# A two-layer attention kernel: the first unit's scores in larger tiles, and an earlier count for the scores made ahead

## What is computed

```python
xn = layernorm(x, g_in)
q = (xn @ Wq).reshape(b, n, H, DH).transpose(0, 2, 1, 3) * scale
k, v = split(xn @ Wkv)            # one head; a null key and value in front
sim = einsum('bhid,bjd->bhij', q, k) + bias
sim = where(causal | padded, -max, sim)
out = einsum('bhij,bjd->bhid', softmax(sim), v)
x = x + layernorm(out.reshape(b, n, H * DH) @ Wo, g_out)
# then the same form again as layer 1
```

## Time and profile before

| what | us |
|---|---|
| median of three runs | 2392.63 (2391.18 to 2395.41) |
| profiled execution | 2398.92 |
| its span | 2397.1 |
| PE busy | 2148.4 |
| DVE, ACT, POOL busy | 1624.3, 1557.8, 1030.0 |

### The profile page before, as it was taken

The page is one execution under the profiler, slowest core; times in us unless marked ns, Lnnn a source line. Parts: engine busy times, 40 slices in busy tenths (PEclk is TensorE's granted clock), DMA queues, the critical chain, the costliest instruction groups (busy, mean ns, idle before and its releaser), DMA issues.

```text
span 2397.1 us, 72132 instructions
## 1 busy us (share of the span) xinstructions
PE 2148.4 (90%) x26395; PEld 1914.7 (80%) x26395; DVE 1624.3 (68%) x3422; ACT 1557.8 (65%) x6241; POOL 1030.0 (43%) x1510
## 2 busy tenths in 40 slices
PE   5898988899988989888999889899899998898987
PEld 4787887788877878877888778778788887787876
DVE  5776766666766767666666666676666666676775
ACT  4676666666666766666666666666666666666765
POOL 3444444444444444444444444444444444444443
PEclk8899999999999999999999999999999999999999
DMA  7121222221222212222212211222122122211211
GB/s 244 50 58 54 63 60 59 63 60 53 58 69 58 57 52 65 57 59 63 60 53 58 69 59 53 55 58 65 59 59 65 53 58 64 59 57 53 69 49 51
DMA packets 183286, 151.60 MB, mean 63 GB/s; under 512 B 121440, under 2 KB 125616, under 8 KB 182992
## 3 DMA queue, kind: packets, MB, share of 16 engines
q1 hardware_dynamic: 181248, 145.77, 20.7%
q0 software_dynamic: 688, 1.14, 0.3%
q10 hardware_dynamic: 1056, 0.00, 0.0%
HBM read 98.56 MB, written 37.77 MB: 57 GB/s over the span
## 4 chain that ended last, share of the span: by engine, by line
PE 84%; issue 8%; DVE 2%; ACT 2%; SPq 1%; POOL 1%; DMA 1%; DVEq 0%; POOLq 0%; ACTq 0%
PE psum L708 31%; PE psum L615 17%; PE psum L581 12%; PE psum L673 9%; PE psum L691 7%; PE psum L543 3%; PE psum L632 2%; PE psum L592 2%; DVE bn_in L1072 1%; SPq L386 1%; ACT qp L870 1%; POOL probs L1474 1%; POOL masked_bias L1464 0%; ACT ln_in L839 0%; ACT probs L900 0%
## 5 line engine op out<-in xcount | busy, mean ns | idle before, releaser
L900 ACT ACTIVATE probs<-probs,neg_max 128x129 f32<-128x129 f32 (+3 forms) x2048 | 712.1, 351 | 76.3 <-DVE neg_max L1140 76.2
L1464 POOL TENSOR_TENSOR masked_bias<-bias,pad_neg 128x516 f32<-128x516 f32 (+3 forms) x512 | 404.1, 821 | 349.0 <-DVE probs L1134 345.3
L1474 POOL TENSOR_TENSOR probs<-probs,den_inv 128x512 f32<-128x512 f32 (+3 forms) x512 | 367.8, 739 | 250.3 <-DVE den_inv L1145 250.3
L1134 DVE TENSOR_TENSOR probs<-psum,masked_bias 128x648 f32<-128x648 f32 x256 | 213.0, 832 | 313.3 <-PE psum L673 312.8
L1486 POOL TENSOR_TENSOR y_out<-y_out,res 128x512 f32<-128x512 f32 x128 | 164.6, 1286 | 554.5 <-ACT y_out L864 554.5
L900 ACT ACTIVATION_READ_ACCUMULATOR probs<-probs,neg_max 128x1 f32 x2048 | 385.9, 188 | 0.0
L1150 DVE STREAM_TRANSPOSE probs_t<-probs 128x512 f32<-128x512 f32 (+3 forms) x512 | 229.9, 487 | 147.3 <-POOL probs L1474 146.3
L708 PE MATMUL psum<-wo_hi,o_hi 128*128 128x512 f32 x1024 | 307.0, 447 | 3.6 <-issue 2.1
L906 ACT ACTIVATE o_hi<-psum,null_v_col 128x512 fp32r<-128x512 f32 x256 | 161.9, 683 | 196.2 <-PE psum L691 196.2
L673 PE MATMUL psum<-keys,q_t 64*64 64x129 f32 (+3 forms) x4096 | 129.6, 265 | 156.0 <-issue 152.9
L708 PE MATMUL psum<-wo_hi,o_lo 128*128 128x512 f32 x1024 | 262.5, 398 | 0.0
(11 more groups left out here) (133 smaller groups left out, 4077.0 us busy)
## 6 DMA issues: line engine op xcount, KB each, us to landing
res<-in_x_dram SPq DMA_DIRECT2D x64, 256.0 KB, 2.8
v_rep<-v_kept SPq DMA_DIRECT2D x512, 32.0 KB, 1.8
x_of<-y_out SPq DMA_DIRECT2D x64, 256.0 KB, 2.1
res<-x_of SPq DMA_DIRECT2D x64, 256.0 KB, 2.8
out_dram<-y_out SPq DMA_DIRECT2D x64, 256.0 KB, 2.1
xa<-in_x_dram SPq DMA_DIRECT2D x63, 256.0 KB, 2.8
xa<-x_of SPq DMA_DIRECT2D x63, 256.0 KB, 2.8
q_aside<-qp SPq DMA_DIRECT2D x32, 256.0 KB, 3.0
```

The source lines that it names most:

```text
L900: x_ = nc.scalar.activation(s, s, ACT.Exp, bias=neg_max[:, b, n:n + 1], accum_out=den[:, b, n:n + 1])
L1134: nc.vector.tensor_tensor(pairs(probs, c), SB[c][:, :, 0:ROW], pairs(masked_bias, c), ALU.add).then_inc(biased[c], 1)
L1464: m = nc.gpsimd.tensor_tensor(block(masked_bias, b), block(bias[u.layer], b), pad_neg[u.layer][:, 0:WIDTH[b]].unsqueeze(1).to_broadcast([P ...
L1474: m = nc.gpsimd.tensor_tensor(some, some, den_inv[:, b, :].unsqueeze(2).to_broadcast([P, 4, n]), ALU.mult)
```

## The change

Two edits on PE alone. In `scores`, the very first unit (layer 0, sequence 0) takes row tiles of 128 instead of 64: 8 matmuls of 64 x 128 a call instead of 16 of 64 x 64, in both of its calls. And the calls with c = 0 of layer-0 units wait for `half_copied` to reach the new number `pfirst`, the count after the first half of the pair's q, instead of `pdone * 2`, the count after both.

```diff
-        return Unit(0, b, u + 1, u, u - 1, n + 1, n, b + 1, odd=b % 2, pdone=b // 2 + 1)
+        return Unit(0, b, u + 1, u, u - 1, n + 1, n, b + 1, odd=b % 2, pdone=b // 2 + 1, pfirst=b // 2 * 2 + 1)
...
-            return Unit(0, two[k], four[2 * k - 1], four[2 * k - 2], four[2 * k - 3], four[x + 1], four[x], two[k + 1], odd=k % 2, pdone=one[k // 2 + 1])
+            return Unit(0, two[k], four[2 * k - 1], four[2 * k - 2], four[2 * k - 3], four[x + 1], four[x], two[k + 1], odd=k % 2, pdone=one[k // 2 + 1], pfirst=two[k // 2 * 2 + 1])
...
                         for k in range(2):
-                            wait(pe, half_copied[k], u.pdone * 2)
+                            wait(pe, half_copied[k], u.pfirst)
...
+                tr = P if static(u, 0, 0) else TR
                 for b in (3, 2, 1, 0):
-                    for r in range(0, P, TR):
+                    for r in range(0, P, tr):
...
-                            m = nc.tensor.matmul(block(SB[c][:, e, :], b)[r:r + TR, :], queries(u, c, half, b)[:, r:r + TR], k,
+                            m = nc.tensor.matmul(block(SB[c][:, e, :], b)[r:r + tr, :], queries(u, c, half, b)[:, r:r + tr], k,
```

More of the change, by code:

```diff
@@ L21, with __init__ @@
 class Unit:
-    def __init__(self, layer, batch, done, prev, before, xdone, xprev, sdone, odd=None, pdone=None, adone=None):
-        self.before = before
+    def __init__(self, layer, batch, done, prev, before, xdone, xprev, sdone, odd=None, pdone=None, pfirst=None, adone=None):
+        self.before, self.pfirst = before, pfirst
         self.layer, self.batch, self.done, self.prev, self.xdone, self.xprev, self.sdone, self.same = (
```

## The result

| | before | after |
|---|---|---|
| time, us (median, 4 runs each) | 2391.94 (2391.18 to 2395.41) | 2149.86 (2148.31 to 2152.80) |
| span of the profiled execution, us | 2397.1 | 2146.5 |
| ratio after to before | | 0.8987, 95% interval 0.8971 to 0.9002 |

The side was right, the size was not.

What follows compares the result with a forecast made beforehand. It took PE, busy 90% of the span, to bound the kernel, with time lost to code loading and a wait on q. Terms 40 + 14 + 39 = 93 to 94 us off 2392.6 gave 2298 us, range 2250 to 2340.

Steps and rivals of the forecast that it cites:

- The edges: Loop body counted in 256-instruction code blocks: old edges at 655, 911 and 1,679, new ones from 207, none near the jump.
- A, the jump: Jump back at the loop's end: its target block fetched alone, about 1.45 us less each, 40 us (11 to 52).
- Rival 1: Block edges don't matter as read, PE's memory holding 2,048 instructions; only the wait's 39 us gained, about 2353 us; chance 0.06.
- B, record 911: Code-loading gap of 0.43 us in the scores that open `second` goes: 14 us, bounds 0 and 20.
- C, half of q: In `second`, PE no longer waits 1.30 us for ACT's copy of q's second half: 39 us, bounds 25 and 42.
- D, the clock: PE's clock, 0.50 granted after each jump, falls as before despite shorter gaps: 0 us, upper bound 45 gained.
- The sum: Whole kernel: 40 + 14 + 39 = 93 to 94 us gained, forecast 2298 us against the median.
- Rival 4: An edge just behind the loop's start makes PE stand again, 3.0 us an iteration, 84 us: 2423 us; chance 0.03.

Runs made afterwards that it cites:

- 128 more: Kernel before with the shorter wait and the first scores call written out three times, 128 instructions more ahead of the loop: 2397.11 us, ratio 1.0028.
- n = 7: Kernel before with the shorter wait and seven pairs of first-call score matmuls joined, 28 instructions fewer ahead of the loop: 2149.40 us, ratio 0.8967.
- n = 6: Kernel before with the shorter wait and six pairs of first-call score matmuls joined, 24 instructions fewer ahead of the loop: 2156.45 us, ratio 0.8996.
- n = 2: Kernel before with the shorter wait and two pairs of first-call score matmuls joined, 8 instructions fewer ahead of the loop: executions 2149.9 and 2170.6 us.

## Why the prediction was wrong, step by step

- **The edges** were counted rightly: with 128 more PE stands a second time behind six matmul records (12 instructions and a few others), where the count has an edge at 15. n = 7 and n = 6, 2 instructions to either side of the edge at the body's end, differ by one whole jump with its nine transfers; that fits, but says less, since n = 2 has a profile without a slow jump too.
- **A, the jump.** This is the step that failed: "The jump's target is then fetched alone." It takes for granted that a target is always fetched. It isn't: in every run here it is kept, as long as the body and the block ahead of it don't exceed eight blocks. And the block in line isn't just "thrown away", as the prediction had it: by the theory it is the one too many. Priced at 40 us; in fact the gap goes but for 0.1 us, 28 x 4.75 = 133 us, as the wait row shows (153.8 to 0.2, 20 of them B's).
- **Rival 1** held the right number, and the prediction turned it down with "the nine transfers an iteration say they don't". The nine transfers fit that number: the body's eight blocks and the one ahead, all reloaded, by the theory, because they are one too many. The size that the Trainium skill gives (Runtime: NRT & Kernel Launch, Instruction fetch mechanics) agrees with the runs at 2,048; 1,705 instructions are under it, but what has to fit is the blocks that they touch and the next. The same section says that a taken branch to a target outside a window of two blocks forces a fetch; here a jump back over six blocks has 0.1 us between the matmuls on its two sides and no transfer, and the measurement decides.
- **B, record 911.** 14 us were forecast, and 14 came: 20 of the gap, less the 6 by which the wait for o_hi grew (1.5 to 7.4), the follower that was named. The reason was wrong, though: the gap is gone since nothing is loaded, not since the edges are spread better. With n = 2 the edges lie 8 instructions from those of before, and PE has no wait on "issue" in front of the scores at all.
- **C, half of q.** 39 us forecast, 41.8 measured between the run with the tiles alone and the changed kernel; the cover of 1.1 us held, and in the loop no wait took its place. While blocks are loaded it is worth 27 (16 to 38), which the prediction didn't see: loading takes a part back.
- **D, the clock.** Put at 0, with 45 as its upper bound. By the two window rows it gives 2.2 us an iteration, 62 us. The clock fell to 0.50 (1.2 GHz) at every gap of 4.5 us or more and stays at 1.00 where there is none. The gap of 3.2 us, for which the prediction had no row, is nearly reached with 128 more: at its gaps of 3.5 to 4.2 us the clock falls too, in the window above for 10.2 us. The bound was too low because it counted the first L708 rows alone.
- **The sum** again: 133 + 14 + 42 + 62 = 251. The terms are read from the two profiled executions, whose spans differ by 2397.1 - 2146.5 = 250.6 us; the medians differ by 242, since the profiled execution before was 7 us above its median and the one after 1.5 below. That 251 meets 250.6 so closely is partly luck: by the two pages of the profile, PE's idle time fell by 183 us (133 + 14 + 42 = 189) and its busy time by 67 (62).
- **Rival 4** never threatened, but is real: 128 instructions more bring the second gap that it described, 2.63 us where it said 3.0, and a kernel a little slower than before even with the wait shortened. (Its 54 us for B and C are 53 by the terms; nothing hangs on it.)

What stays open: which block gives way to the ninth, and why one jump that finds its target is followed by none that doesn't. No run looks into the memory itself. That seven blocks and the one ahead stay, and eight by themselves, is shown by loops without a transfer; that nine don't fit is inferred from the nine transfers of every slow iteration, and that the oldest is dropped is only argued. No run ends a body far enough into its eighth block for the ninth to be there before the jump.

## What to carry to other kernels

Count a loop body in blocks of 256 instructions from the edge, and with it the block behind its last: on PE, up to eight in all were free here, and nine cost 3.5 to 5.2 us at every jump, stalls in fast stretches and half the clock for 3 to 10 us around each. The sign to look for is a number of instruction transfers that grows with the iterations; if it does, moving the loop by a few dozen instructions in code that runs once, either way, may be worth more than any work on the body. Price a wait only after that, since what one saves while code is loading comes back in part at the next edge.

## What was unexpected in the hardware

- A jump back over 1,700 instructions costs next to nothing where the body is loaded: 0.1 us on PE's timeline, against 4.5 to 5 us.
- A body that ends 2 to 22 instructions behind an edge can start slow and become fast within one execution, and then stays so; how late differs from one execution to the next (18 behind: 2149.9 and 2170.6 us; 22 behind: 2174.0 and 2308.2, the last without a profile). The time of such a kernel can't be told from one run.
- One jump's reload costs more in the clock and in followers than it looks: 7.0 us in the two iterations compared (71.6 and 64.6), where the gap itself is 5.0.
